# Twelve products of a dense item in one step of the attention, the step without a value product

## The reference, cut to what matters

```
q, k, v = x @ wq.T, x @ wk.T, x @ wv.T            # per batch, 256 x 512
q, k    = rotary(q), rotary(k)
p       = softmax(causal(q k^T / 4))              # per batch and head, 256 x 256
y       = layernorm(x + (p v) @ wo.T)
gate,up = (y / 128) @ w_gate.T, (y / 128) @ w_up.T      # 1376 wide
i8      = trunc(clip(silu(gate) * up * 128, -128, 127))
out     = layernorm(y + trunc(clip((i8 @ w_down.T) * 128, -128, 127)))
```

## Time and profile before

| | us |
|---|---|
| median of 3 runs | 385.71 (385.07 to 385.84) |
| the profiled execution | 385.31 |
| its span | 383.5 |
| TensorE busy | 358.1 (93%) |
| VectorE busy | 261.1 (68%) |
| ScalarE busy | 205.6 (54%) |
| GpSimd busy | 104.1 (27%) |

### The profile page before, as it was taken

The page is one execution under the profiler, slowest core; times in us unless marked ns, Lnnn a source line. Parts: engine busy times, 40 slices in busy tenths (PEclk is TensorE's granted clock), DMA queues, the critical chain, the costliest instruction groups (busy, mean ns, idle before and its releaser), DMA issues.

```text
span 383.5 us, 7266 instructions
## 1 busy us (share of the span) xinstructions
PE 358.1 (93%) x2458; PEld 276.0 (72%) x2458; DVE 261.1 (68%) x926; ACT 205.6 (54%) x387; POOL 104.1 (27%) x111
## 2 busy tenths in 40 slices
PE   7989797999999898997999998999999999999991
PEld 4876565677777676774777776888888888878881
DVE  5748887587679778797447368766555565457775
ACT  5876386776839676596443552563434433322220
POOL 4122024231334222471331201353332223120011
PEclk9999996999999999999999999999999999999997
DMA  7959779569491868929800400123112200001111
GB/s 261 361 96 180 141 95 168 66 111 180 56 172 27 127 147 129 218 56 204 196 9 3 169 1 2 55 68 98 45 41 78 82 27 27 2 1 55 56 55 55
DMA packets 79841, 37.59 MB, mean 98 GB/s; under 512 B 68672, under 2 KB 72896, under 8 KB 79808
## 3 DMA queue, kind: packets, MB, share of 16 engines
q1 hardware_dynamic: 76928, 35.08, 41.3%
q10 hardware_dynamic: 2880, 2.10, 3.0%
HBM read 17.24 MB, written 2.10 MB: 50 GB/s over the span
## 4 chain that ended last, share of the span: by engine, by line
PE 74%; DVE 8%; ACT 5%; DMA 4%; issue 4%; POOL 2%; SPq 1%; ACTq 1%; POOLq 0%; DVEq 0%
PE bank L889 7%; PE bank L891 6%; PE bank L890 6%; PE s_pair L889 5%; PE st_pair L889 5%; PE bank L1006 5%; PE s_pair L891 5%; PE s_pair L890 5%; PE st_pair L891 5%; PE st_pair L890 5%; DMA QT<-QS 3%; PE st_pair L989 3%; PE bank L1106 3%; PE bank L1107 3%; DVE SM L676 2%
## 5 line engine op out<-in xcount | busy, mean ns | idle before, releaser
L466 ACT ACTIVATE PTS<-st_pair 128x384 f32<-128x384 f32 x128 | 57.7, 489 | 37.1 <-PE st_pair L992 32.1
L676 DVE CUSTOM_DVE_ANT_0 SM<-s_pair,K 128x128 bf16<-128x128 f32 (+1 forms) x172 | 52.5, 352 | 22.4 <-PE s_pair L974 22.3
L346 POOL TENSOR_TENSOR RQ<-RQ,QS 128x256 f32<-128x256 f32 x32 | 22.6, 707 | 90.2 <-ACT QS L443 90.2
L331 POOL TENSOR_TENSOR GL<-gu_raw,GH 128x1024 fp32r<-128x1024 f32 x11 | 27.0, 2452 | 68.7 <-ACT GH L506 68.7
L592 ACT ACTIVATE f_a<-f_c 128x512 f32<-128x512 f32 x22 | 13.9, 632 | 57.0 <-DVE f_c L816 57.0
L989 PE MATMUL st_pair<-identb,maskb 128*128 128x256 bf16 x128 | 35.9, 280 | 5.8 <-ACT PTS L466 3.1
L676 DVE CUSTOM_DVE_ANT_0 SM<-bank,K 128x128 bf16<-128x128 f32 x84 | 26.5, 353 | 13.5 <-PE bank L974 13.5
L889 PE MATMUL s_pair<-YH,GH 128*128 128x512 f32 x80 | 31.4, 393 | 0.0
L889 PE MATMUL st_pair<-YH,GH 128*128 128x512 f32 x80 | 31.2, 390 | 0.0
L891 PE MATMUL s_pair<-YH,GL 128*128 128x512 f32 x80 | 31.1, 389 | 0.0
L891 PE MATMUL st_pair<-YH,GL 128*128 128x512 f32 x80 | 31.1, 389 | 0.0
(11 more groups left out here) (147 smaller groups left out, 941.7 us busy)
## 6 DMA issues: line engine op xcount, KB each, us to landing
gu_raw<-wgu SPq DMA_DIRECT2D x11, 512.0 KB, 3.8
w_raw<-wqkvo SPq DMA_DIRECT2D x6, 512.0 KB, 9.0
wd_raw<-wd SPq DMA_DIRECT2D x11, 256.0 KB, 3.0
RES<-x SPq DMA_DIRECT2D x4, 512.0 KB, 5.0
out<-o SPq DMA_DIRECT2D x8, 256.0 KB, 2.0
XR<-xT SPq DMA_DIRECT2D x3, 512.0 KB, 4.5
w_raw<-wqkvo ACTq DMA_DIRECT2D x4, 256.0 KB, 4.6
QT<-QS SPq DMA_TRANSPOSE x64, 3.8
```

Source lines behind the costliest of these rows:

```text
L466: nc.scalar.activation(PTS[:, (2 * p + half) % R_PTS, :], st_pair[:, half, 0:SW], ACT.Exp, scale=-1.0).then_inc(S["pr"], 1)
L676: last = nc.vector.tensor_tensor_reduce(out=SM[:, (2 * p + half) % 3, cols], in0=bS[(2 * p + half) % 3][:, cols], in1=above, scale=1.0, sc ...
```

## The change

Every four-chunk item now has `i[5]` = 1: its twelve products stand together in its first step. The items that started in an even step, or took three steps, get new places:

- third and fourth projection of the last batch: steps 39 and 41 (before 37 to 39 and 40 to 42);
- output projection, first half, of batch 1: step 45 (before 44 to 46);
- the two value projections of the last batch: 49 and 51 (before 48 to 49, 50 to 51);
- turned rows 0 to 3: 52 to 55 (before 51 to 54);
- gate, up, gate, up: 57, 58, 59, 60 (before 56 to 57, 57 to 58, 59 to 60, 60 to 61).

All others keep their first step, which is odd, and lose their second. `outp 1` of batch 2 stays at 63 and 64, the turned rows 4 and 5 at 67 and 68. `ended` takes a four-chunk item to end one step after its start, so ScalarE and VectorE read most items in the same steps as before, now one step after TensorE has done them.

```diff
     if b:
-        DENSE += [("outp", 1, b - 2, 1, g - 1, 2)] if b > 1 else []
+        DENSE += [("outp", 1, b - 2, 1, g - 1, 1)] if b > 1 else []
     if b + 2 < B:
-        DENSE += [("proj", m, b + 1, m % 2, g + 1 + 2 * m, 2) for m in range(6 if b else 4)]
+        DENSE += [("proj", m, b + 1, m % 2, g + 1 + 2 * m, 1) for m in range(6 if b else 4)]
     elif b + 1 < B:
-        DENSE += [("proj", m, b + 1, m % 2, g + at, n) for m, at, n in ((0, 1, 2), (1, 3, 2), (2, 5, 3), (3, 8, 3))]
+        DENSE += [("proj", m, b + 1, m % 2, g + at, 1) for m, at in ((0, 1), (1, 3), (2, 7), (3, 9))]
     else:
-        DENSE += [("proj", 4, b, 0, g, 2), ("proj", 5, b, 1, g + 2, 2)]
-        DENSE += [("yt", t, 0, t % 2, g + 3 + t, 1) for t in range(NTT // 2)]
-        DENSE += [("gate", 0, 0, 0, g + 8, 2), ("up", 0, 0, 1, g + 9, 2), ("gate", 1, 0, 0, g + 11, 2), ("up", 1, 0, 1, g + 12, 2)]
+        DENSE += [("proj", 4, b, 0, g + 1, 1), ("proj", 5, b, 1, g + 3, 1)]
+        DENSE += [("yt", t, 0, t % 2, g + 4 + t, 1) for t in range(NTT // 2)]
+        DENSE += [("gate", 0, 0, 0, g + 9, 1), ("up", 0, 0, 1, g + 10, 1), ("gate", 1, 0, 0, g + 11, 1), ("up", 1, 0, 1, g + 12, 1)]
     if b:
-        DENSE += [("outp", 0, b - 1, 0, g + 13, 2) if b != B - 2 else ("outp", 0, b - 1, 0, g + 12, 3)]
+        DENSE += [("outp", 0, b - 1, 0, g + 13, 1)]
...
 def ended(g):
-    return [i for i in DENSE if i[5] and i[4] + i[5] - 1 == g]
+
+    return [i for i in DENSE if i[5] and i[4] + max(i[5], 2 if chunks(i) == NC else 1) - 1 == g]
```

## The result

The changed kernel is slower: 388.00 us median (387.84 to 388.14, 4 runs) against 385.39 (384.75 to 385.84, 4 runs), ratio 1.0085, interval 1.0046 to 1.0123. I forecast 384.3 and a range to 387.5; the sign was wrong, and the time lies outside.

What follows compares the result with a forecast made beforehand. TensorE, busy 358.1 of 383.5 us, was taken as the bound in some stretches, chains of waits in others. Terms sum to -1.35 us: 383.96 against the profiled execution, 384.3 as median; range 382.1 to 387.5.

Steps and rivals of the forecast that it cites:

- Part one: TensorE's dense products: twelve in one run save a run start, 0.17 us per item; a pair of steps 5.49 us for 5.66.
- Part two: Maxima in eight steps (21 to 57) lose their cover of six dense products and wait for VectorE's transpose: 3.8 us.
- about 12 and 6: Sign of being right: TensorE's maxima wait for VectorE's transpose about 12 times and 6 us, up from 4 and 2.4 us.
- a gain in 53: Step 53: turned rows start one step later, so VectorE has no low part ahead of its transpose; within a +0.2 us term.
- Part three: What moves in the stretches with slack, priced one by one, from -1.6 us to +0.35 us per stretch.
- steps 37 to 39: Step 37 without dense work, all twelve in 39, whose shifted scores need the maxima of 37: 8.5 us against 8.14, +0.35.
- The half clock: Rival: bare steps 37, 38 and 43, 44 bring a second half-clock stretch, up to 3.5 us, 387.8 us; chance 0.06.
- Steps 40 to 46: Twelve and a wait of 0.4 in 41, 43 and 44 paced by VectorE, 45's twelve after the maxima: +0.25 us.
- Steps 1 to 8: Fourth projection all in step 7 leaves 1.5 us less behind the DMA wait, against score-bank waits: -0.8 us (-1.5 to +0.2).
- 17 to 36, 47 to 55: Run starts saved against maxima waits in 17 to 32 (-0.15), 33 to 36 (+0.25); 47, 48 shorter (-1.6); 49 to 55 +0.2 us.
- 9 to 16: No dense item before or after, mean granted clock 0.81; the stretch moves as a whole: 0 us.
- 56 to 62: Five runs instead of seven in part, -0.25, and one maxima wait, +0.4: +0.15 us.

Runs made afterwards that it cites:

- the last version: The changed kernel with the items of 33, 35 and 41 split and the maxima after the shifted scores: 381.86 us, ratio to the kernel before 0.9895.

## Why the prediction was wrong, step by step

- **Part one, twelve together: right.** 5.47 us a pair for a forecast 5.49, so nothing extra shows from the value product to the scores.
- **Part two, cover of the maxima: right in place, and in size by the sum.** From the first scores to the maxima, seven of the eight steps take 0.73 or 0.74 us for the 0.34 of a covered step, and step 57 takes 1.24: together 3.7 us of new waits for a forecast 3.8. The profile's own figure, 11 waits of 4.1 us for "about 12 and 6", is lower because it marks only 0.24 us of each 0.40. The sum is right in part by luck: 33, 37 and 49 were taken at 0.6 and cost 0.4, and step 57, taken at 0.4, costs 0.90 (marked 0.74). The low part of the last turned rows, moved one step later with them, stands on VectorE just ahead of that transpose, the same effect that I counted as a gain in 53 and overlooked in 57:
```profile
182.67 0.69 DVE L737 TENSOR_TENSOR YL<-bank,YH 128x512 fp32r<-128x512 f32 x1
183.27 0.44 DVE L697 STREAM_TRANSPOSE OTT<-bank 128x256 f32<-128x256 f32 x1
...
183.86 0.27 PE L961 MATMUL bank<-identb,MP 128*72 128x128 bf16 x2 [0.74 <-DVE OTT L697]
```
- **Part three, steps 37 to 39: the step that failed.** Forecast +0.35, measured +2.61. I worked the stretch out as TensorE's products and one chain of 4.2 us from the maxima of 37 to the shifted scores of 39, and took ScalarE to be free for the maxima as in the earlier trace rows; I had written that ScalarE's reading of items "is off the path and costs 0". Measured, that term is 5.88 us (126.69 to 132.57), and the profile marks no wait for the DMA at its end: TensorE's stop of 1.45 us for ScalarE in step 38 and the slow value product fill it. Step 39 from there on takes 4.13 us for a forecast 3.36, partly at half clock. ScalarE's exponentials are fed by TensorE once a step. A run of twelve in 33 or 35 makes them wait 1.3 to 1.8 us while ScalarE's list for the pieces is full, and ScalarE brings that lateness into the two steps that the change had left without dense work. The half clock, a rival of mine at 0.06 as a cause by itself, came behind the stop, and made about 1 us of it.
- **Steps 40 to 46**: forecast +0.25, measured +0.92, by the same cause in 41 and 44 (0.6 us; with 41 split 43 to 46 take 10.33 instead of 10.91). Item 45, for which the prediction has no price of its own, costs 0.22.
- **Steps 1 to 8**: forecast -0.8, measured -0.23. I had allowed for one more wait for the score banks; there are three (0.41, 0.79 and 0.41 us, in 3, 5 and 7) where the kernel before had one (0.49, in 5), since VectorE takes 2.3 us for two pairs' scores (36.11 to 38.42) and a bare step lasts 0.34.
- **17 to 36, 47 to 55**: -0.15, +0.25, -1.6 and +0.2 forecast, -0.01, +0.18, -1.32 and -0.21 measured. The slack behind 49 was real: with only the items from 47 on changed, 47 to 55 take 25.34 us for 26.93.
- **9 to 16**: 0 forecast, -0.34 measured. This stretch took 16.77 to 20.39 us in versions with the same work there, so it says nothing of the change. Its time doesn't follow the clock alone either: 17.65 us at a granted clock of 1.00 in the version with only the first projections changed, and 16.77 at 0.90 in the one with only 17 to 32 changed.
- **56 to 62**: forecast +0.15, measured +0.60, most of it by step 57 (part two).

The missed terms, 2.26 in 37 to 39, 0.67 in 40 to 46, 0.57 in 1 to 8 and 0.45 in 56 to 62, are 3.95 us. The two traces are 2.58 us apart where I forecast -1.35, a distance of 3.93; the other terms and the later start of step 1 cancel.

Two loose ends. The version with both 33 and 35 split ends 1.2 us above its expectation though its stretch does not; its trace has that much in steps 9 to 16. And the kernel before with later maxima is slower by its ratio while its trace isn't. There the executions tell: the four at a mean granted clock of 0.988 or 0.989, the profiled one among them, took 384.26 to 384.65 us, and the eight at 0.985 or less 385.23 to 388.49. Why half-clock periods come more often in one version than in another stays open. So does the share of each part in the 1.0% of the last version: 33, 35 and 41 split without the later maxima was not run.

## What to carry to other kernels

Where one engine feeds another once a step, the length of the step is the other's supply interval: joining work saves its starts (0.17 us each here) and can starve the fed engine by about as much as the work ahead of its feed grew: here 1.34 us more of dense products (2.82 for 1.48), and 1.34 to 1.41 us more of idle time before the exponentials. Before moving work, add up the fed engine's own list against the time between its feeds, over all steps up to the next bare one, not in the changed step alone. And move a synchronising instruction behind independent work before taking its cover away: in this kernel later maxima with three items left split ended 1.0% below the kernel before, where the joining alone lost 0.8%. A lesson from one kernel, not a rule that was tested on another.

## What the runs showed of the hardware

A stop of TensorE of 1.2 to 1.6 us in step 38, without dense products, was followed by a period at granted clock 0.5 in six of seven versions that had it (the value product behind it took 0.95 to 1.51 us for 0.86); the seventh, with later maxima, stayed at full clock. No version with a stop of 0.5 us or less there had one. It is a tendency and no rule: every trace has a stop of 1.2 to 1.5 us in step 14, and a half-clock period began in step 14 or 15 in 15 of the 20 traces, in step 16 in one and not at all in four. The same work can have its half-clock period in other places: the part from step 63 to the last output DMA took 178.0 to 178.2 us in all versions but one, and there 179.8, with such a period in it.

What such a period costs shows in step 56: 4.75 to 4.82 us with it, 3.26 in the kernel before. Over whole executions of the kernel before, a mean granted clock of 0.985 instead of 0.994 goes with 2.4 us (medians 385.37 and 383.01).
